# The row maxima of attention: turned by VectorE in square blocks and placed by four transfers, where TensorE and ScalarE turned them

## The reference

```python
x = x + xattn(layernorm(x), ctx, Wq, Wk, Wv, Wo, bo)
#   q, k, v: 16 heads of 64;  attn = softmax(q @ k.T / 8);  out = (attn @ v) @ Wo + bo
x = x + ffn(layernorm(x), router_w, w1, b1, w2, b2)
#   scores = softmax(x @ router_w); each of 8 experts takes its 513 best rows,
#   y = gelu(rows @ w1 + b1) @ w2 + b2, times the score, added back to those rows
```

## Time and profile before

| | |
|---|---|
| median of 3 runs | 1377.65 us (1377.4 to 1378.37) |
| profiled execution | 1379.35 us |
| its span, first to last instruction | 1377.5 us, mean granted TensorE clock 0.976 |
| busy in the span: TensorE, VectorE, ScalarE, GpSimd | 94%, 74%, 59%, 65% |
| prologue, attention (from, to) | 0 to 77, 77 to 1044 us |

### The profile page before, as it was taken

How to read it: one execution, slowest core, us unless ns; L and a number is a source line. 1 busy time by engine, 2 the same in 40 slices (tenths; PEclk the granted TensorE clock), 3 DMA queues, 4 the chain that set the end, 5 groups by cost and what they waited for, 6 DMA issues and landing times. The chain is left out here.

```text
span 1377.5 us, 24906 instructions
## 1 busy us (share of the span) xinstructions
PE 1299.5 (94%) x8340; PEld 817.2 (59%) x8340; DVE 1025.2 (74%) x1676; ACT 806.6 (59%) x1093; POOL 893.9 (65%) x463
## 2 busy tenths in 40 slices
PE   7989999999999999999999999999999926999996
PEld 5655555555555555555455555555447915999996
DVE  5767878787887788788777877877977775666662
ACT  5456666666666666566566666666663213657753
POOL 3347876886787688779678877877687002445553
PEclk9999999999999999999999999999999956999998
DMA  9530010002001100200010010001313441545422
GB/s 258 200 128 10 25 42 31 17 18 63 17 24 31 45 17 17 60 21 17 26 57 17 16 57 24 17 17 63 127 53 116 162 155 58 142 133 128 105 37 28
DMA packets 75863, 88.83 MB, mean 64 GB/s; under 512 B 10555, under 2 KB 55644, under 8 KB 75740
## 3 DMA queue, kind: packets, MB, share of 16 engines
q1 hardware_dynamic: 68956, 78.32, 17.5%
q0 software_dynamic: 6784, 8.94, 4.0%
HBM read 58.98 MB, written 27.99 MB: 63 GB/s over the span
## 5 line engine op out<-in xcount | busy, mean ns | idle before, releaser
L919 POOL TENSOR_TENSOR acc_p<-acc_p,x_in 128x1024 f32<-128x1024 f32 x192 | 487.6, 2539 | 131.6 <-ACT x_in L1019 124.6
L100 DVE TENSOR_REDUCE mx_part<-ps_m 128x1 f32<-128x512 f32 x552 | 362.9, 685 | 178.5 <-PE ps_m L81 176.7
L1019 ACT ACTIVATE x_in<-ps_s 128x1024 f32<-128x1024 f32 x384 | 380.3, 1024 | 98.1 <-PE ps_s L835 71.3
L847 PE MATMUL ps_o<-x_in,v 128*64 128x512 f32 x1664 | 406.2, 606 | 0.3 <-DMA v<-v_scr 0.3
L824 PE MATMUL ps_s<-q,k 64*128 64x512 f32 x2496 | 386.4, 395 | 0.9 <-ACT x_in L1019 0.9
L824 PEld LDWEIGHTS ps_s<-q,k 64*128 64x128 f32 x2496 | 273.2, 185 | 41.7 <-ACT x_in L1019 6.6
L81 PE MATMUL ps_m<-k,q 64*128 64x512 f32 x736 | 211.6, 454 | 8.0 <-PEq L216 3.2
L847 PEld LDWEIGHTS ps_o<-x_in,v 128*64 128x64 f32 x1664 | 99.5, 136 | 180.9 <-issue 142.1
L81 PEld LDWEIGHTS ps_m<-k,q 64*128 64x128 f32 x736 | 99.5, 184 | 144.9 <-issue 100.8
L919 DVE TENSOR_TENSOR acc_d<-acc_d,x_in 128x1024 f32<-128x1024 f32 x96 | 174.8, 1821 | 5.8 <-ACT x_in L1019 5.5
L691 ACT ACTIVATE kept<-ps_m 128x512 f32<-128x512 f32 x184 | 109.6, 596 | 48.0 <-PE ps_m L81 45.3
(11 more groups left out here) (256 smaller groups left out, 1946.6 us busy)
## 6 DMA issues: line engine op xcount, KB each, us to landing
w_in<-in_w SPq DMA_DIRECT2D x16, 1024.0 KB, 5.1
v_st<-rec_scr SPq DMA_DIRECT2D x64, 128.0 KB, 2.9
o_scr<-v_st SPq DMA_DIRECT2D x32, 256.0 KB, 2.1
v<-v_scr SPq DMA_DIRECT2D x8, 832.0 KB, 5.3
v_scr<-c_in SPq DMA_DIRECT2D x10, 512.0 KB, 3.7
c<-o_scr SPq DMA_DIRECT2D x2, 1792.0 KB, 8.3
x_in<-in_x SPq DMA_DIRECT2D x4, 512.0 KB, 9.8
k<-o_scr SPq DMA_DIRECT2D x1, 2048.0 KB, 8.1
```

What stands on the lines that cost most here:

```text
L100: dve.tensor_reduce(part[:, j // S.MF, j % S.MF:j % S.MF + 1], bank[:, 0:S.MC], AX.X, ALU.max).then_inc(done or G.rough_used[hd], 1)
L847: last = pe.matmul(ps_o[hd * HP:hd * HP + DH, :], v[b][:, s, hd * DH:(hd + 1) * DH], probs[:, g % RING, hd * QC:(hd + 1) * QC], start=(s = ...
L919: eng.tensor_tensor(acc, other, probs[:, (u * KT + t) % RING, :], ALU.add).then_inc(done, 1)
L1019: act.activation(probs[:, g % RING, :], ps_s[:, g % 2, :], ACT.Exp, bias=G.pad_bias[:, 0:1] if s == KT - 1 else 0.0, scale=SCALE).then_inc ...
```

## The change

The new `turn_max` runs on VectorE at slot 9 where `dve_max` reduced: it reduces into the first 8 columns of a tile `mx` of 128 x 32 whose other columns are zero, waits for that result, waits until the transfers of the hand-over before have read `mx_t`, and transposes `mx` into `mx_t` in four blocks of 32 x 32. Of each block, 8 partitions hold 32 queries each of the 8 rows. `place_mrow` places a block with one transfer, of 8 pieces of 32 values, so four per hand-over. The transpose on TensorE, the copy on ScalarE, and their waits and bank entry go; the sign moves into `ones_row`, which now holds -1.

```diff
+BLOCK, BLOCKS = 32, P // 32
 def place_mrow(sp, S, G, buf):
-    half = P // 2
-    for hd in range(2):
-        sp.dma_start(raw(G.m_rows[hd * half:hd * half + 1, buf, :]), raw(G.m_row[hd * S.QT:(hd + 1) * S.QT, :])).then_inc(G.mrow_placed, 16)
+    rows = raw(G.m_rows[0:P:P // 2, buf, :]).rearrange("o (t b r) -> o t b r", b=BLOCKS, r=BLOCK)
+    for i in range(BLOCKS):
+        sp.dma_start(rows[:, :, i, :], G.mx_t[i * BLOCK:i * BLOCK + 2 * S.QT, :]).then_inc(G.mrow_placed, 16)
+def turn_max(S, G, dve, unit):
+    dve.tensor_reduce(G.mx[:, 0:2 * S.QT], G.mx_part[:], AX.X, ALU.max).then_inc(G.max_ready, 1)
+    dve.wait_ge(G.max_ready, unit + 1)
+    if not (isinstance(unit, int) and unit == 0):
+        dve.wait_ge(G.mrow_placed, 16 * BLOCKS * unit)
+    dve.transpose(G.mx_t[:], raw(G.mx[:])).then_inc(G.mrow_ready, 1)
...
         BANK_USE = ("v0 v1 v2 v3 k0 k1 v4 k2 k3 v5 v6 v7 v8 v9 q0 v10 q1 v11 q2 v12 q3".split()
-                    + [f"v{n}" for n in range(13, len(vjobs) - 3)] + ["mx"] + [f"v{n}" for n in range(len(vjobs) - 3, len(vjobs))])
+                    + [f"v{n}" for n in range(13, len(vjobs))])
...
-                    pool.memset(raw(G.ones_row[hd * HP:hd * HP + 1, :]), 1.0).then_inc(s_ones, 1)
+                    pool.memset(raw(G.ones_row[hd * HP:hd * HP + 1, :]), -1.0).then_inc(s_ones, 1)
                     pool.wait_ge(s_ones, 8 + hd)
+                pool.memset(raw(G.mx[:]), 0.0).then_inc(s_ones, 1)
...
-                dve.tensor_reduce(G.mx[:], G.mx_part[:], AX.X, ALU.max).then_inc(G.max_ready, 1)
-                dve.wait_ge(G.max_ready, 1)
+                dve.wait_ge(s_ones, 10)
+                turn_max(S, G, dve, 0)
...
-                    if n == len(vjobs) - 3:
-                        act.wait_ge(G.maxt_ready, 1)
-                        act.activation(G.m_row[:], bank("mx")[0:2 * S.QT, 0:P], ACT.Copy, scale=-1.0).then_inc(G.mrow_ready, 1)
...
-                    if n == len(vjobs) - 3:
-                        pe.wait_ge(G.max_ready, 1)
-                        bank_free(pe, "mx")
-                        pe.transpose(bank("mx")[0:2 * S.QT, 0:P], G.mx[:], ident[:]).then_inc(G.maxt_ready, 1)
...
         def x_wait(pe, p, u, s, last):
             users = [((a, DEN_SLOT), den_copied, UNITS * p + a) for a in range(1 if first else 0, UNITS)]
-            users += [((a, MROW_SLOT), mrow_ready, UNITS * p + a + 2) for a in range(UNITS)]
             users += [(at, stage_lo, proj_count(p, n) + 1) for n, at in enumerate(PROJ_PLACES) if proj_here(n, first, last)]
-            users = [((-1, MROW_SLOT), mrow_ready, UNITS * p + 1)] + [x for x in users if x[0] < (u, s)]
-            at, copied, count = max(users, key=lambda x: x[0])
-            pe.wait_ge(copied, count)
+            users = [x for x in users if x[0] < (u, s)]
+            if not first:
+                users.append(((-1, 0), stage_lo, PROJ_JOBS * p - 1))
+            if users:
+                at, copied, count = max(users, key=lambda x: x[0])
+                pe.wait_ge(copied, count)
...
             dve.wait_ge(kept_read, len(KEPT) * unit - sum(k < MAHEAD for k in KEPT))
-            wait_for(dve, maxt_ready, unit)
-            dve.tensor_reduce(mx[:], G.mx_part[:], AX.X, ALU.max).then_inc(max_ready, 1)
-        def pe_maxt(pe, unit):
-            pe.wait_ge(max_ready, unit + 1)
-            pe.transpose(ps_x[0:NMU, 0:P], mx[:], G.ident[:]).then_inc(maxt_ready, 1)
-        def act_mrow(act, unit):
-            act.wait_ge(maxt_ready, unit + 1)
-            wait_for(act, mrow_placed, 32 * unit)
-            act.activation(m_row[:], ps_x[0:NMU, 0:P], ACT.Copy, scale=-1.0).then_inc(mrow_ready, 1)
+            turn_max(S, G, dve, unit)
...
             if s == 0:
-                pe.wait_ge(mrow_placed, 32 * (unit + 1))
+                pe.wait_ge(mrow_placed, 16 * BLOCKS * (unit + 1))
```

More of the change, by code:

```diff
@@ L565 @@
 DIFF_KEEP = ((1, 8), (2, 0), (2, 8))
-DEN_SLOT, MROW_SLOT = 4, 10
+DEN_SLOT = 4
 MAX_SLOT, REC_SLOT, NORM_ADD = 9, 7, 6
@@ L608, in phase_attention @@
     SCALE = float(DH) ** -0.5
-    NMU = 2 * S.QT
     ND, NPL = len(DVE_TILES) - 1, len(POOL_TILES) - 1
@@ L621, in phase_attention @@
         den_c, rec_c = G.den_c, G.rec_c
-        mx, m_row = G.mx, G.m_row
         o_n = G.v_st[:, 0, :].rearrange("p (a q) -> p a q", a=2)
@@ L645, in phase_attention @@
         rough_ready, rough_used = G.rough_ready, G.rough_used
-        max_ready, maxt_ready, mrow_ready = G.max_ready, G.maxt_ready, G.mrow_ready
+        max_ready, mrow_ready = G.max_ready, G.mrow_ready
         proj_ready, stage_hi, stage_lo = sem("proj_ready"), sem("stage_hi"), sem("stage_lo")
@@ L972, in small @@
                     pe_proj(pe, PROJ_PLACES.index((u, s)), p + 1)
-                if s == MROW_SLOT and not (last and u == UNITS - 1):
-                    x_wait(pe, p, u, s, last)
-                    pe_maxt(pe, unit + 1)
             for u in range(UNITS):
@@ L1034, in copies @@
                     act_diff(act, DIFF_HI.index((u, s)), 1 - b, p)
-                if s == MROW_SLOT and not (last and u == UNITS - 1):
-                    act_mrow(act, unit + 1)
             def rough(u, s):
@@ L2135, in build @@
                 G.mx_part = sb("mx_part", [P, S.UQ // P, 4], F32)
-                G.mx, G.m_row = sb("mx", [P, 2 * S.QT], F32), sb("m_row", [2 * S.QT, P])
-                G.max_ready, G.maxt_ready, G.mrow_ready, G.mrow_placed = (
-                    sem(n) for n in ("max_ready", "maxt_ready", "mrow_ready", "mrow_placed"))
+                G.mx, G.mx_t = sb("mx", [P, BLOCK]), sb("mx_t", [P, BLOCK], F32)
+                G.max_ready, G.mrow_ready, G.mrow_placed = (
+                    sem(n) for n in ("max_ready", "mrow_ready", "mrow_placed"))
                 G.rough_ready = [sem(f"rough_ready{hd}") for hd in range(2)]
```

## The result

The changed kernel takes 1375.54 us (median of 22 runs, 1374.22 to 1377.6), the kernel before 1378.45 in the same series (22 runs, 1376.54 to 1382.38). The ratio is 0.998 with an interval of 0.9974 to 0.9985: 2.9 us or 0.2% faster. The forecast was a gain of 5.1 us. The direction is right, the size is little over half.

A forecast was written before the change was run, and what follows sets the result against it. TensorE, busy 358.4 of 360 us in attention, was taken to set the pace. The terms -6.15 + 0.25 + 0.8 = -5.1 us took the runs' median of 1377.65 to 1372.6 us, range 1370.4 to 1376.6.

The forecast's parts named there:

- TensorE's transposes, -6.15: Attention loop: 30 of 31 removed TensorE transposes save 0.205 us each, 6.15 us in all.
- if half the hand-overs sit ahead of another engine's chain, 3.1: Attention loop: lower bound on TensorE's saving, 3.1 us instead of 6.15.
- the 38 waits of the earlier trace: Attention: TensorE's weight loads wait for VectorE 38 times, 28.8 us; most called no stall, just a group start's 0.81 us.
- VectorE, +0.25: Slot 9: VectorE's new transpose makes it late eight times by about 0.03 us, 0.25 us lost.
- The formula of the prediction's rival paragraph: VectorE's transpose: 58 cycles and one per column at 0.96 GHz, 0.09 us, no lateness, 0.25 us less in the sum.
- ScalarE, 0: Attention loop: removing 31 ScalarE copies of 0.27 us gains nothing, since what follows waits for TensorE's later matmuls.
- The row in the loop, 0: Loop hand-over: four SP transfers instead of two cost nothing, with 5.6 us left to land.
- the prediction's 2.0 us: Row transfers: a fixed 2.0 us each, mostly completion; with completions overlapped it changes nothing in the sum.
- The prologue, +0.8: Prologue's end: four SP issues taking 2.8 us send the last store of v 0.8 us later.
- half-gain rival: Attention loop: VectorE's chain sets the period, half the gain stays, -2.05 us, 1375.6; chance 0.15, shared with no gain.
- second rival: Hand-over: two TensorE waits per unit, 0.05 us of each exposed, give 1.6 us more; 1370.0 with cheap prologue issues; chance 0.08.
- its own range: Whole kernel: the forecast's range from its prologue and VectorE bounds, 1370.9 to 1375.0 us around 1372.6.

The follow-up runs named there:

- e2: Changed kernel with a constant TensorE transpose put back at slot 10 of units 2 and 3: 1379.68 us, 1.0006 of the kernel before.
- e6: As e5, with constant TensorE transposes also put back at slot 10 of units 0 and 1: 1384.24 us, 0.997 of the kernel before.
- e1: Changed kernel with a constant TensorE transpose put back at slot 10 of units 0 and 1: 1375.86 us, 0.9979 of the kernel before.
- e5: Changed kernel with one GpSimd subtraction of unit 1 cut to 32 columns, the rest left out: 1383.01 us, 0.9966 of the kernel before.
- e7: Changed kernel; unit 0's second-head rough score of slot 11 issued behind that slot's first two products: 1384.59 us, 0.9977 of the kernel before.
- e3: Kernel before with VectorE's transpose and its two waits added at slot 9, on a tile nobody reads: 1379.34 us, 1.0002 of the kernel before.
- e8: Changed kernel with the prologue's four row transfers issued one store of v earlier: 1384.59 us, 0.9976 of the kernel before.
- e9: The changed kernel again, unaltered, in the last series: 1376.31 us, 0.9985 of the kernel before.
- e10: Changed kernel with the edits of e7 and e8 together: 1373.54 us, 0.9964 of the kernel before.

## Why the forecast was right in sign and off in size

**TensorE's transposes, -6.15: the step that failed.** The price of one was right: the next load moves by 0.20, and a transpose put back costs about 0.2 where it costs anything (0.18 and 0.21 in e2, 0.24 in unit 1 of e6). The count was wrong. From the first unit to the last attention takes 934.45 us where it took 937.78: 3.3 us, not 6.15. Two hand-overs of every four give their 0.2, and the other two at most about 0.05 each, as the table, e1 and e2 show. My bound for this case, "if half the hand-overs sit ahead of another engine's chain, 3.1", was nearly the number; I gave its rival 0.15. The sentence that dismissed it was that VectorE waits for TensorE behind nearly every hand-over, "so its chain starts earlier too". VectorE does start earlier (255.71), but a chain that begins early helps only if nothing fixed stands in it. Behind the hand-over stands GpSimd's work, which was released before it (by the trace) and holds VectorE (shown by e5 and e6). And I had counted as real stalls only those of the last pair: the 0.38 at 262.75, which stands with 0.38 to 0.44 in each of the first seven pairs, was among the 38 waits of the earlier trace rows and I passed over it because most of them were the harmless 0.81.

**Unit 0** was no stall at all before. The second head's bank came free while TensorE transposed; with 0.2 us less in between, the wait shows (e7). No row of before could show it as a wait, but VectorE's operations at 221.10 and 221.55 are the two that stand ahead of that reduction.

**VectorE, +0.25: 0 by e3.** The duration was right (0.19 taken, 0.211 measured, bound 0.29). Reduction to transpose is 0.20 to 0.31 us from start to start in 29 of 32 cases and 0.65 in three, so the wait on its own result mostly took 0.13 us, not the 0.04 of the prediction. Behind the transpose VectorE still idles in 25 of 32 cases; in unit 2 of six pairs and once in the last pair it no longer does, as forecast, and by e3 nothing follows from it. The timeline of unit 1:

```profile
248.12 0.17 DVE L101 TENSOR_REDUCE mx<-mx_part 128x8 fp32r<-128x32 f32 x1
248.42 0.21 DVE L105 STREAM_TRANSPOSE mx_t<-mx 128x32 f32<-128x32 f32 x1
249.20 0.69 DVE L112 TENSOR_REDUCE mx_part<-ps_m 128x1 f32<-128x512 f32 x1 [0.57 <-PE ps_m L81]
```

The formula of the prediction's rival paragraph, an estimate of 0.09 us from the Trainium skill (VectorE: DVE Perf Modes, The TRN2 errata), is less than half of what was measured. The same section says that its 58 cycles under-predict and that about 150 were measured; that makes the estimate 0.19 us, a little nearer than the neighbouring reduction's 0.17.

**ScalarE, 0.** Nothing speaks against it, but no run had ScalarE's copy alone, so it isn't shown by itself. **The row in the loop, 0:** right; TensorE's loads at L831 wait for no transfer from 80 to 1050 us. (The section of the Trainium skill behind the prediction's 2.0 us is on transfers of GpSimd's path; these go by SP's queue, and nothing here measured how long one takes to land.)

**The prologue, +0.8: +0.52,** since the four issues take 2.31 us, not 2.8. The mechanism was right, and e8 takes it away.

**The sum** with the measured terms is -3.3 + 0 + 0.5 = -2.8 us. The runs say 2.9, with an interval of 2.1 to 3.6, and 1.8 when repeated (e9; 0.8 to 3.3). That the two agree to 0.1 is luck, as the open point below shows. The 1372.6 for the likeliest was 2.9 too low: 2.1 of that is the smaller gain, and the rest is the kernel before, which took 1378.45 in this series and not 1377.65. So it is luck, too, that the half-gain rival's 1375.6 is the measured time: its gain was 2.05, and the measured one lies between it and the forecast. Two workings of the prediction were off without bearing on this. Two waits of 0.05 us in 31 units are 3.1 us, not the 1.6 of the second rival, and the bounds named for "its own range" give 1371.1 to 1374.5, not 1370.9 to 1375.0.

**Open.** The profiled execution of after is 3.6 us shorter than that of before, and not all of it is in the sum: its first unit starts 1.0 earlier, the units up to the last take 3.3 less, and what follows the last unit's start takes 0.7 more (361.9 against 361.2; 362.2 in e9 and 361.1 in e10). The earlier start comes from ahead of the hand-over of the prologue. The first reduction to mx starts at 67.33 us in before and 67.71 in e3, which has before's prologue, and at 65.19 to 66.70 in after and the nine other runs; from there to the end of the last copy of v it is 6.94 us both before and after. The largest difference on the way is ScalarE's wait until a store of v has landed and its buffer is free. Before and after:

```profile
38.14 0.60 ACT L411 ACTIVATE c_in<-pro_ps 128x512 f32<-128x512 f32 x1 [3.80 <-DMA v_scr<-c_in]
```

```profile
35.20 0.60 ACT L424 ACTIVATE c_in<-pro_ps 128x512 f32<-128x512 f32 x1 [0.88 <-DMA v_scr<-c_in]
```

It is 3.40 in e3 and at most 1.89 in the others. Whether the change makes this store land sooner or it is scatter of single executions is not shown. It is why spans of two profiles are a poor measure of a gain of this size, and units, which repeat within 0.07 us, a good one.

## What to carry to other kernels

Removing work from the engine that is busy all the time pays only up to the next wait on a chain that this engine doesn't release. So for each removed piece, go from its place to the next wait of that engine, however short, and ask what the other engine was doing then and who released it, back to before the removed piece. A stall that recurs once per period, even one of 0.4 us, takes back what was gained since its chain was released, as unit 2 did with the 0.2 of unit 1. And a gain of tenths per unit is better read from the distance of one repeated instruction than from the whole time.

## What the runs showed of the hardware

VectorE's addition of two SBUF tiles of 128 x 1024 takes 1.2 us alone and, at the same place of e5, before and after, 1.42, 1.96 and 2.23 beside GpSimd's. Its end is what is fixed: 1.09 us behind the end of GpSimd's instruction in all three. It waits for GpSimd's instruction to end, whenever it was issued itself. The hold is mutual: GpSimd's operation on v_st takes 2.25 to 2.29 us where VectorE's addition is under way (256.82 above, ending at 259.07, 1.13 behind VectorE's), and 1.27 in six of the twelve units of before's window. These are the groups of it in the 360 us window, before and after (count, busy us, mean ns, idle ahead):

```profile
L898 POOL TENSOR_TENSOR v_st<-v_st 128x512 f32<-128x512 f32 x12 | 21.2, 1764 | 0.0
```

```profile
L894 POOL TENSOR_TENSOR v_st<-v_st 128x512 f32<-128x512 f32 x12 | 27.2, 2267 | 0.0
```

The operation is the same, but it lasts 0.5 us longer on average: after the change VectorE's addition is in its way in all twelve units, before in six. So a busy time that rises on an engine whose work wasn't touched is a hint at an operation that is held. It accounts for 6.0 of the 7.2 us by which GpSimd's busy time grew in the window (277.95 in the earlier trace rows, 285.14 after).
